# A table of gather units, paired distance tiles and a matching order on GpSimd, in a fused attention and nearest-neighbour kernel

## What is computed

```python
# first layer, in chunks of 64 columns
scores = einsum('bnqhd,bnkhd->bnhqk', qh, kh) * scale + where(mask > 0, 0, NEG)
out = einsum('bnhqk,bnkhd->bnqhd', softmax(scores), vh) @ W_out.T + b_out
y = layernorm(out * mask + x)
# second layer
pd = 2 * einsum('bdn,bdm->bnm', p, p) - xx[:, :, None] - xx[:, None, :]
idx = top_k(pd, 30)[1]
rel = pts[bidx, idx] - pts[:, :, None, :]
rho, theta, phi = sqrt(r2), arctan2(z, sxy), arctan2(y, x)
feat = concat([sph, sph - mean(sph)])      # then three layers with batch norm -> att
result = y + einsum('bnkc,bnk->bnc', y_k, softmax(att))
```

## Time and profile before

| | |
|---|---|
| median of three runs | 5790.62 us |
| profiled execution | 5790.79 us, span 5788.7 us |
| busy in the span: VectorE | 5127.8 us, 89% |
| TensorE | 4476.3 us, 77% |
| ScalarE | 4035.6 us, 70% |
| GpSimd | 3045.6 us, 53% |
| granted TensorE clock, mean | 0.874 |

### The profile page before, as it was taken

How to read it: one execution, slowest core, us unless ns; L and a number is a source line. 1 busy time by engine, 2 the same in 40 slices (tenths; PEclk the granted TensorE clock), 3 DMA queues, 4 the chain that set the end, 5 groups by cost and what they waited for, 6 DMA issues and landing times. The chain is left out here.

```text
span 5788.7 us, 168877 instructions
## 1 busy us (share of the span) xinstructions
PE 4476.3 (77%) x62610; PEld 2718.6 (47%) x63182; DVE 5127.8 (89%) x7549; ACT 4035.6 (70%) x9505; POOL 3045.6 (53%) x3780
## 2 busy tenths in 40 slices
PE   5777777777777777777777777776395889999999
PEld 2444444444444444444444444443242666666666
DVE  7999989999989999998999998997398988888887
ACT  3777777777777777777777777776533766676666
POOL 3577777777777777777777777776400000000000
PEclk7888888888888898888888888887697899999999
DMA  0010000010000001000001000000000000000000
GB/s 29 16 31 16 16 17 16 17 31 16 17 16 17 17 16 32 16 17 16 17 17 31 17 16 17 16 16 12 1 0 8 25 30 27 30 26 30 26 30 26
DMA packets 135798, 114.60 MB, mean 20 GB/s; under 512 B 105344, under 2 KB 106112, under 8 KB 134784
## 3 DMA queue, kind: packets, MB, share of 16 engines
q1 hardware_dynamic: 134912, 102.73, 6.1%
HBM read 69.16 MB, written 33.55 MB: 18 GB/s over the span
## 5 line engine op out<-in xcount | busy, mean ns | idle before, releaser
L866 DVE MAX8 vals<-pd_sb 128x8 f32<-128x1024 f32 x1024 | 1200.6, 1211 | 302.2 <-ACT pd_sb L588 284.0
L588 ACT ACTIVATE ohT<-oh_ps 128x512 bf16<-128x512 f32 x1920 | 1152.0, 615 | 155.3 <-PE oh_ps L482 114.4
L871 DVE FIND_INDEX8 idx<-vals,pd_sb 128x8 uint16<-128x1024 f32 x1024 | 1244.6, 1218 | 0.0
L503 PEld LDWEIGHTS g_ps<-tparts,ohT 128*128 128x128 bf16 x23040 | 871.8, 99 | 380.9 <-issue 148.7
L503 PE MATMUL g_ps<-tparts,ohT 128*128 128x24 bf16 x23040 | 883.9, 175 | 81.6 <-issue 33.5
L873 DVE MATCH_REPLACE8 pd_sb<-vals,pd_sb 128x1024 f32<-128x1024 f32 x768 | 928.3, 1209 | 0.0
L1957 PEld LDWEIGHTS e_a_ps<-planes,e_oh 120*128 120x128 bf16 x24576 | 687.9, 97 | 299.5 <-issue 218.4
L482 PE MATMUL oh_ps<-bitsT,code 128*128 128x512 bf16 x1348 | 590.3, 442 | 293.4 <-ACT bitsT L772 155.7
L1727 ACT COPY e_at<-e_a_ps 128x512 f32<-128x512 f32 x512 | 543.1, 1061 | 356.1 <-PE e_a_ps L1957 349.8
L1957 PE MATMUL e_a_ps<-planes,e_oh 120*128 120x32 bf16 x24576 | 702.4, 178 | 83.2 <-DVE e_oh L1885 46.9
L754 ACT ACTIVATE sS<-s_ps,mx 128x64 f32<-128x64 f32 x2048 | 611.5, 329 | 169.4 <-DVE mx L896 168.1
(11 more groups left out here) (241 smaller groups left out, 7411.3 us busy)
## 6 DMA issues: line engine op xcount, KB each, us to landing
ctx_s<-in_ctx SPq DMA_DIRECT2D x32, 512.0 KB, 4.2
maskb<-in_mask_Bx1x_ff SPq DMA_DIRECT2D x32, 512.0 KB, 6.7
x_s<-in_x SPq DMA_DIRECT2D x32, 512.0 KB, 5.8
y_spill<-y_s SPq DMA_DIRECT2D x32, 512.0 KB, 3.0
e_y<-y_spill SPq DMA_DIRECT2D x32, 512.0 KB, 3.9
out<-e_o SPq DMA_DIRECT2D x64, 256.0 KB, 2.2
table<-in_ctx SPq DMA_DIRECT2D x96, 4.0 KB, 5.8
pd_sb<-in_shape_constants SPq DMA_DIRECT2D x1, 1180.0 KB, 5.4
```

Source lines behind the costliest of these rows:

```text
L503: m = nc.tensor.matmul(found_ps[gi % 2][:, k % GK, t, :], ohT[:, k % OHR, bass.ts(t, P)], tparts[:, par, part, :], start=(part == 0), stop ...
L588: return nc.scalar.activation(dst, src, func, scale=scale, bias=bias)
L866: nc.vector.max(vals[:, i, :], pd_sb[:, (t + i) % RING, :]).then_inc(topk_step, 1)
L871: found = nc.vector.max_index(idx16[:, par, t + i, 8 * r:8 * r + 8], vals[:, i, :], work)
```

## The change

Three things change in stage a.

1. A table `units_at` gives the number of units in each of the eight places of the four slots of a half. The slots get 5, 9, 7 and 9 units. Slots 0 and 4 have none in their first two places.
2. The distances of tiles t+2 and t+3 are both made in slot t for even t: t+2 where it stood, t+3 in two halves around the seventh place, in which the even slots have no unit. Odd slots make no distances.
3. The rest follows the shift. ScalarE's angles and squares go from slot 2 to 1, its roots from 4 to 5; GpSimd's `sph_turn` and `sph_signs` from slot 3 to 2, `sph_denoms` from 5 to 6; group 2 of each half is taken in slot 3 or 7 rather than 2 or 6; the split of the next batch's norms (`squares_split`) goes from slot 4 to 5; VectorE's reciprocal (`denoms`) stands after round 3 instead of round 1 of the last pair.

```diff
-        unit_starts = (0, 7, 15, 22, 30)
-        slot_groups = [(4, 5), (0,), (1, 2), (3,)]
+        units_at = ((0, 0, 1, 1, 1, 1, 0, 1),
+                    (1, 1, 1, 1, 1, 2, 0, 2),
+                    (1, 1, 1, 1, 1, 1, 0, 1),
+                    (1, 1, 1, 1, 1, 2, 0, 2))
+        unit_starts = [sum(sum(row) for row in units_at[:n]) for n in range(QT + 1)]
+        slot_groups = [(4, 5), (0,), (1,), (2, 3)]
...
@@ TensorE's emit
-                    unit()
-                    ahead(0)
-                    unit()
-                    ahead(1)
-                    unit()
+                    units(0)
+                    if t % 2 == 0:
+                        ahead(2, 0)
+                    units(1)
+                    if t % 2 == 0:
+                        ahead(2, 1)
+                    units(2)
                     if quarter < QT - 1:
                         scores(b, par, t + 1)
...
-                    unit()
+                    units(3)
                     if before:
                         probs_in = turn_probs(misc, b if t > 0 else b - 1, (t - 1) % TILES)
-                    unit()
+                    units(4)
                     if before:
                         moved = values(misc, (t - 1) % TILES, probs_in)
-                    unit()
+                    units(5)
+                    if t % 2 == 0:
+                        ahead(3, 0)
+                    units(6)
+                    if t % 2 == 0:
+                        ahead(3, 1)
                     if quarter == 0 and before:
                         rows(misc, moved)
...
-                    unit()
-                    unit()
+                    units(7)
...
@@ ScalarE's emit (its places as TensorE's)
-                    if t == 2:
+                    if t == 1:
                         if there(b - 3):
                             angles(b - 3)
                         if there(b - 2):
                             rel_squares(b - 2)
-                    if t == 4 and there(b - 2):
+                    if t == 5 and there(b - 2):
                         roots(b - 2)
...
@@ VectorE
-                        if t == 6 and r == 1 and there(b - 2):
+                        if t == 6 and r == 3 and there(b - 2):
                             denoms(b - 2)
...
@@ GpSimd's emit
+                        if not last:
+                            gate(pool, y_ready, b * 2 + 1, pool_gates)
+                            squares_split(b + 1, 1 - par, misc_base(b) + (12 if first else 16))
...
-                    if t == 3:
+                    if t == 2:
                         if there(b - 3):
                             sph_turn(b - 3)
                         if there(b - 2):
                             sph_signs(b - 2)
-                    if t == 5 and there(b - 2):
+                    if t == 6 and there(b - 2):
                         sph_denoms(b - 2)
...
-                        squares_split(b + 1, 1 - par, misc_base(b) + (12 if first else 16))
+                        gate(pool, minv_ready, b + 2, pool_gates)
```

More of the change, by code:

```diff
@@ L272, in stage_a @@
         NG = QUADS * GROUPS
-        unit_starts = (0, 7, 15, 22, 30)
-        slot_groups = [(4, 5), (0,), (1, 2), (3,)]
+        units_at = ((0, 0, 1, 1, 1, 1, 0, 1),
[3 rows of a table added]
+        unit_starts = [sum(sum(row) for row in units_at[:n]) for n in range(QT + 1)]
+        assert unit_starts[QT] == K
+        slot_groups = [(4, 5), (0,), (1,), (2, 3)]
         FILLS = 31
@@ L513, in emit, with units, ahead @@
                     at = unit_starts[quarter]
-                    end = unit_starts[quarter + 1]
-                    def unit():
+                    def units(place):
                         nonlocal at
-                        if not first and at < end:
-                            gather(b - 1, 1 - par, h, at, at + 1, turned)
-                        at += 1
-                    def ahead(half):
-                        if t + 2 < TILES:
-                            distances(b, par, t + 2, half)
+                        n = units_at[quarter][place]
+                        if not first and n > 0:
+                            gather(b - 1, 1 - par, h, at, at + n, turned)
+                        at += n
+                    def ahead(tiles, half):
+                        if t + tiles < TILES:
+                            distances(b, par, t + tiles, half)
                         elif not last:
-                            distances(b + 1, 1 - par, t + 2 - TILES, half)
+                            distances(b + 1, 1 - par, t + tiles - TILES, half)
                     before = t > 0 or not first
@@ L676, in emit, with units, ahead @@
                     at = unit_starts[quarter]
-                    end = unit_starts[quarter + 1]
-                    def unit():
+                    def units(place):
                         nonlocal at
-                        if not first and at < end:
-                            gather(b - 1, h, at, at + 1)
-                        at += 1
-                    def ahead(half):
-                        if t + 2 < TILES:
-                            distances(b, par, t + 2, half)
+                        n = units_at[quarter][place]
+                        if not first and n > 0:
+                            gather(b - 1, h, at, at + n)
+                        at += n
+                    def ahead(tiles, half):
+                        if t + tiles < TILES:
+                            distances(b, par, t + tiles, half)
                         elif not last:
-                            distances(b + 1, 1 - par, t + 2 - TILES, half, normed)
+                            distances(b + 1, 1 - par, t + tiles - TILES, half, normed)
                     before = t > 0 or not first
@@ L918, in squares_split @@
             def squares_split(b, par, moved):
-                gate(pool, minv_ready, b + 1, pool_gates)
                 gate(pool, misc_moved, moved, pool_gates)
@@ L1139, in _ @@
             invert(0, 0, 0)
+            pool.wait_ge(minv_ready, 1)
             squares_split(0, 0, 2)
```

## The result

The changed kernel takes 6011.57 us (median of four runs, 6004.69 to 6021.27); the kernel before took 5789.44 us beside it (5787.87 to 5792.64). The ratio is 1.0384, 95% interval [1.0368, 1.0399]: 222 us slower. I had forecast slower, but 5847 us, and the range ended at 5950.

What follows compares the result with a forecast made beforehand. ScalarE's chain was taken to bind: 121.6 + 12.0 - 8.8 + 3.0 + 2.0 = 129.8 us a batch, taken as 128.1 for the clock. +1.85 over 30 batches gave 5847 us, range 5680 to 5950.

Steps and rivals of the forecast that it cites:

- Signs (1) to (3), (5) and (6): Profile after: MAX8 wait under 2 us, `mx` 9 or more, `pd_sb` 70 or more, table-to-exponents under 2, ScalarE-for-maxima under 10.
- Sign (4): Copies `gsb` waiting for GpSimd: from 25.0 to about 55 us in 1000, two of some 3.5 us a batch.
- The base, 126.25 - 4.7: ScalarE's chain left to itself: a batch without its 4.7 us wait for VectorE's score maxima, 121.6 us.
- (a): Even slots: two distance halves back to back lengthen ScalarE's chain by 3.0 to 5.4 us, four times; 12.0 taken.
- (b): Slots 0 and 4: exponents sooner after the bit table, 8.8 us less a batch; `pT` later, 3.0 more.
- (d): At nothing: moved units, table functions (angles, squares, roots), `denoms`, `squares_split`, added gates; TensorE waits up to 7 us at worst.
- the first rival: Full clock: ScalarE's pauses on TensorE shrink, 123.8 to 125.8 us a batch, 5717 to 5777 us; chance 0.27.
- (c): GpSimd, slots 3 and 7: copy of group 4 waits for group 2, 7.0 us a batch; net +2.
- the second way through the signs run: Slot 3: slot 2's normalisation through `sph_signs` to group 2's end, 31.5 us; ends like `kt`'s path or up to 7 later.
- VectorE's pace: Second rival: VectorE binds, batch falls to 117.9 us plus a few, 5540 or up to 5705 us; chance 0.12.
- the cancelled sum: Third rival: gain and loss cancel, 5780 to 5802 us; chance 0.07.
- The fourth: Fourth rival: pairs at slow pitch, 6.6 us, in two of four slots or more, or `squares_split` late; 5935 up; chance 0.06.

Runs made afterwards that it cites:

- the first experiment: Changed kernel with group 2 put back in slots 2 and 6 and `sph_turn` and `sph_signs` back in slot 3: 6013.4 us, ratio 1.0389.
- both GpSimd edits: Changed kernel with group 2 back in slots 2 and 6 and the signs run cut in two, halves back to back: 5739.24 us, ratio 0.9917.
- the fastest version: Changed kernel with group 2 back, a unit between the halves, and the signs run cut between slots 2 and 4: 5686.43 us, ratio 0.9811.
- the singles: Changed kernel with only group 2 back in slots 2 and 6: 5896.92 us; with only the signs run cut in two: 5988.93 us.

## Why the prediction was right and wrong

**The frame was right.** ScalarE's chain sets the pace, VectorE does not; the direction follows from it. Signs (1) to (3), (5) and (6) came as written: MAX8 waits 1.2 us a batch (under 2 us); `mx` waits 11.7 (9 or more); `pd_sb` 89.5 (70 or more); from the bit table to the exponents 1.5 us (2076.16 to 2077.64, under 2; the mean is 2.0); ScalarE's wait for the maxima is gone (under 10). Sign (4) came in kind: `gsb` waits 46.5 in 16 times, two a batch of about 3, forecast about 55 with two of 3.5.

**The sum failed, by 5.0 us a batch (128.1 forecast, 133.1 measured).** By its steps:

- The base, 126.25 - 4.7: right.
- (a) and the wait in (b) together: 12.0 for four pairs, less the 2.04 us in front of the half at the bit table, twice, makes 7.9. Measured +6.6 (`pd_sb`). Right within the estimate.
- (b) failed. The exponents did come 4.3 us sooner after the bit table (6.3 before and 2.0 after, in the mean), but of the 8.8 us only what was waiting could shorten the chain. Those were the 4.1 for the halves and 1.8 for the units beside them: 0.48 and 0.21 in slot 4, in the two rows below, which stand between the bit table and the half of the earlier trace rows, and 0.87 and 0.21 in slot 0 of the same batch. The other 2.9 were ScalarE's busy time for three units, twice, which it now spends in another slot; it is busy for 94.2 us a batch before and after. I subtracted elapsed time where only waiting can be saved: 2.9 us too low.

```profile
2084.84 1.09 ACT L588 ACTIVATE ohT<-oh_ps 128x512 bf16<-128x512 f32 x2 [0.48 <-PE oh_ps L482]
2086.13 0.60 ACT L588 ACTIVATE ohT<-oh_ps 128x512 bf16<-128x512 f32 x1 [0.21 <-PE oh_ps L482]
```

- The largest error is a term of (d), put at nothing because "the units only change slots". Their waits for TensorE were to fall by the 1.8 in (b) and rose by 6.1: 7.9 us too low. A unit's fill now stands on TensorE behind scores that take up to 1.98 us. The two experiments with one part alone say where this comes from: in slots 0 and 4 the units wait 0.3 us a slot before, 1.9 in the changed kernel, 2.4 with the table alone and 0.3 with the pairing alone; in slots 1 and 5 it is 0.3, 1.6, 0.4 and 1.5 (means from 1000 to 3900 us, counted from the exponents of a slot to those of the next). So the table makes the first, with its units behind the exponents, and the pairing the second, with no distance half left beside the scores. I named such pauses against the first rival, and gave them no term.
- `pT`: forecast +3.0 in (b) and about -2 in (c), +1.0; measured -3.1. `y_s`, -1.8, was not forecast.
- (c), the groups: 7.0 - 3.2 = +3.8 forecast, +3.0 measured. Against the old order the net of +2 was near (0 by the first experiment). But what it says of the kernel was wrong. The two edits there move more than the whole loss: cutting the signs run and returning group 2 gives 272 us, 9.1 a batch, and I had called the second way through the signs run equal to the first and stopped there. Two equal ways are not one price: each hides the other.
- The clock: I let it give back 1.7, and it gave back nothing. Two neighbouring batches before have 0.86 and 0.89 (2001.07 to 2127.32 and the next; the earlier trace rows is near the higher one), the two after 0.82 and 0.86, and over the whole span it went from 0.874 to 0.853. I had also read most digits of the earlier trace rows as 0.7 to 0.8; they are 8, which is 0.8 and above. No run here held the clock full, so its own share of the loss is not measured; the trace shows that the mean of one scores matmul went from 704 to 788 ns (rows at the end). The Trainium skill ("TensorE: Matmul & The Clock Gate", Part 1, The HAM clock gate) puts the ramp's penalty under 1% of a typical kernel's span. The prediction applied this to all time at the lower clock, which is more than the sentence says, and came to 5774; the time went the other way.

In sum the errors are +2.9 (b), +7.9 (units), +1.7 (clock), -4.1 (`pT`), -1.8 (`y_s`), -1.3 (`pd_sb`), -0.8 (groups): +4.5 of the 5.0. That the 5.0 is no more is luck in part: `pT` and `y_s` came out 5.9 lower than I had them. Over 30 batches the measured +6.85 makes 206 of the 222 us. The rest is the choice of batches: in the mean from 1000 to 3900 us a batch goes from 125.5 to 132.9 us, +7.5, which makes 224.

This is a sum of waits, not of prices. With both GpSimd edits ScalarE still waits about as long for distances and units (88.5 and 81.1), and the kernel is 49 us faster than the one before. So the terms that I mis-sized can stand in a kernel that is not slower; what brought it below is the order on GpSimd, in slots 3 and 7.

The table functions in (d) were wrong too, as far as they were tried: the later roots gain 75 us in the kernel before, and cost 98 beside the pairing (5777.71 to 5875.34).

**The rivals.** Full clock, VectorE's pace and the cancelled sum are all refuted by a batch of 133.1 us. The fourth, 131 us and above, has the right time by luck and the wrong reason: the pairs run at the fast pitch of 2.10 us, and TensorE has no wait for the norm split in the view of waits.

**Open.** Why table and pairing gain 10 and 13 us alone and lose 29 together, and why the later roots gain 75 us alone and lose 98 beside the pairing, is not settled. For the first, the slot of 25.3 us that the kernel with table and pairing has (2103.69 to 2128.95) holds a wait of 1.50 for the normalisation behind the signs run, and most of it is other waits. Which engine gives the pace in the fastest version, whose neighbouring batches differ by 4.4 us, was not tested.

## What to carry to other kernels

Count what a reordering removes from an engine's chain in waits only; the busy time of a moved instruction comes back wherever it goes, and the check is that the engine's busy time for one batch stays the same. When work is dealt out anew, ask of every long run on another in-order engine (here 15.6 us on GpSimd) which urgent instruction stands behind it in its new slot, and cut it before moving it. When two late things stand on one engine, undo both before judging either: here the singles gave 115 and 23 us, the two together 272.

## What was not expected of the hardware

TensorE's speed changes from tile to tile within a batch. The groups of TensorE instructions by line, 2000 to 3000 us, first of the kernel before and then after (count, busy us, mean ns of one, idle before):

```profile
L444 PE MATMUL s_ps<-kz,qs 128*64 128x512 f32 x254 | 79.1, 704 | 0.0
```

```profile
L449 PE MATMUL s_ps<-kz,qs 128*64 128x512 f32 x240 | 84.2, 788 | 0.0
```

The pause just before does not decide it: in the kernel after the scores at 2115.79 take 1.08 us behind a pause of 1.38, those at 2082.67 1.98 behind one of 1.00. The granted clock of the span was 0.882 with the table alone, 0.862 with the pairing alone, 0.853 in the changed kernel and 0.880 in the fastest, so the pairing goes with a lower clock where nothing else differs. It does not order the kernels by time: the later roots had 0.867 at 5715 us, the kernel before 0.874 at 5790.
